# Audio tower on one core: the second chunk's tokens and first norm inside the first chunk's scan, and norm steps ahead of scans

## The reference

```python
h = einsum('bnp,dp->bnd', patches, W) + b                 # tokens
x = layernorm(h)                                          # "ln1"
u = rmsnorm(x, rms1_w) @ in_proj_w.T                      # z, xv, B, C, dt_in
dt = softplus(dt_in @ dt_proj_w.T + dt_proj_b)
dA = exp(dt[..., None] * A); dBx = (dt * x_full) * B
for each step: s = dA * s + dBx; y = C . s                # 10 steps, 16 states a channel
y = (y + D_skip * x_full) * silu(z)
r = x + y @ out_proj_w.T
h = h + r + (silu(rmsnorm(r) @ gate.T) * (rmsnorm(r) @ up.T)) @ down.T     # "rms2"
h = h + (silu(ln(h) @ wg.T) * (ln(h) @ wu.T)) @ wd.T                       # "ln2"
```

## Time and profile before

| | us |
|---|---|
| median of 3 runs | 675.78 (672.87 to 676.73) |
| the profiled execution, its own time | 675.06 |
| its span in the profile | 673.3 |
| PE busy in the span | 631.5 |
| POOL, DVE, ACT busy | 429.2, 418.0, 346.4 |

### The profile page before, as it was taken

How to read it: one execution, slowest core, us unless ns; L and a number is a source line. 1 busy time by engine, 2 the same in 40 slices (tenths; PEclk the granted TensorE clock), 3 DMA queues, 4 the chain that set the end, 5 groups by cost and what they waited for, 6 DMA issues and landing times.

```text
span 673.3 us, 8617 instructions
## 1 busy us (share of the span) xinstructions
PE 631.5 (94%) x2846; PEld 505.7 (75%) x2846; DVE 418.0 (62%) x532; ACT 346.4 (51%) x773; POOL 429.2 (64%) x244
## 2 busy tenths in 40 slices
PE   4969998799999989999979999999999999999998
PEld 3736765466665757777747777766999998999998
DVE  4077896889887879889887888851322223332132
ACT  4359889358989364434356433422542442653441
POOL 0176785437786999987877987644455463445461
PEclk9879998799999989999989999999999999999999
DMA  8699997489999969988866898533443453134421
GB/s 340 238 365 364 318 299 268 141 258 357 350 373 348 390 250 349 413 336 318 320 247 257 320 330 323 191 125 122 138 149 126 125 157 126 63 130 132 146 67 44
DMA packets 49164, 163.50 MB, mean 243 GB/s; under 512 B 4320, under 2 KB 18528, under 8 KB 48480
## 3 DMA queue, kind: packets, MB, share of 16 engines
q1 hardware_dynamic: 49120, 162.95, 68.9%
HBM read 145.24 MB, written 17.69 MB: 242 GB/s over the span
## 4 chain that ended last, share of the span: by engine, by line
PE 75%; DVE 11%; ACT 5%; POOL 3%; issue 3%; DMA 2%; SPq 0%; DVEq 0%; ACTq 0%; POOLq 0%
PE work L992 54%; PE da L992 15%; DVE da L784 6%; PE work L1002 5%; DVE hs L794 3%; POOL hs L447 2%; ACT L522 2%; ACT da L548 1%; DMA bb<-b_rows 1%; DMA c_rows<-c_rows 1%; DMA sm<-small 0%; POOL hs L460 0%; DVE a L849 0%; ACT z L665 0%; DVE work L809 0%
## 5 line engine op out<-in xcount | busy, mean ns | idle before, releaser
L784 DVE TENSOR_TENSOR_SCAN da<-da,hs 128x580 f32<-128x580 f32 (+1 forms) x128 | 191.1, 1493 | 39.6 <-POOL hs L447 22.2
L447 POOL TENSOR_TENSOR hs<-dtx,bb 128x1160 f32<-128x1160 f32 (+1 forms) x64 | 171.2, 2677 | 61.1 <-PE work L1002 54.1
L426 POOL TENSOR_TENSOR ws<-wraw,ws 128x1024 fp32r<-128x1024 f32 x40 | 101.4, 2536 | 92.8 <-ACT ws L557 92.8
L992 PE MATMUL work<-sq,wraw 128*128 128x290 f32 x512 | 125.7, 406 | 1.1 <-DVE sq L882 1.1
L992 PE MATMUL work<-hn,win 128*128 128x290 f32 (+1 forms) x336 | 104.4, 459 | 16.6 <-DVE hn L857 8.1
L992 PEld LDWEIGHTS work<-sq,wraw 128*128 128x128 f32 x512 | 96.5, 189 | 30.0 <-issue 1.6
L548 ACT ACTIVATE da<-dt,a_neg 128x261 f32<-128x261 f32 (+1 forms) x256 | 118.2, 493 | 0.0
L794 DVE TENSOR_TENSOR hs<-da,cb 128x580 f32<-128x580 f32 (+1 forms) x128 | 105.2, 822 | 10.7 <-DMA cb<-c_rows 2.7
L992 PEld LDWEIGHTS work<-hn,win 128*128 128x128 f32 x336 | 65.5, 200 | 50.7 <-issue 26.0
L545 ACT COPY da<-zeros 128x58 f32<-128x58 f32 (+1 forms) x128 | 27.6, 216 | 126.0 <-DVE hs L794 125.8
L557 ACT CAST ws<-wraw 128x1024 fp32r<-128x1024 f32 x48 | 50.3, 1048 | 70.2 <-PE da L992 34.4
(11 more groups left out here) (98 smaller groups left out, 655.2 us busy)
## 6 DMA issues: line engine op xcount, KB each, us to landing
wraw<-w_stream SPq DMA_DIRECT2D x104, 512.0 KB, 4.1
bb<-b_rows SPq DMA_DIRECT2D x32, 700.0 KB, 7.1
cb<-c_rows SPq DMA_DIRECT2D x32, 700.0 KB, 5.6
bb<-b_rows SPq DMA_DIRECT2D x32, 580.0 KB, 8.0
cb<-c_rows SPq DMA_DIRECT2D x32, 580.0 KB, 6.0
c_rows<-c_rows SPq DMA_DIRECT2D x8, 875.0 KB, 10.8
c_rows<-c_rows SPq DMA_DIRECT2D x8, 725.0 KB, 6.6
win<-w_in SPq DMA_DIRECT2D x4, 1024.0 KB, 13.4
```

The source lines that it names most:

```text
L426: nc.gpsimd.tensor_tensor(ws[:, k % NW, 1, :], wraw[:, split_loads[k] % NRAW, :], ws[:, k % NW, 0, :].bitcast(F32), ALU.subtract).then_inc ...
L447: nc.gpsimd.tensor_tensor(hs[:, u % NH, 0:NQ * n].rearrange("p (n t) -> p n t", t=n), dtx[:, t % 2, 0:n].unsqueeze(1).to_broadcast([P, NQ, ...
L784: nc.vector.tensor_tensor_scan(da[:, j, 0:w], da[:, j, 0:w], hs[:, u % NH, j * w:(j + 1) * w], 0.0, ALU.mult, ALU.add).then_inc(scan_done, 1)
L992: last = nc.tensor.matmul(dst, w, x, start=(k == 0), stop=(k == len(pairs) - 1))
```

## The change

- Chunk 1's tokens are four steps of one product each, in slots 5, 6, 8 and 9, at the front of slots that hold chunk 0's projections; `mean` is put into slot 10, `ln1` into 11, `rms1` into 13. All but `rms1` are now `LATE`. The squares are kept in `th` and `acc`, which are idle in chunk 0's scan, the norm's results in `rstd` and `rstd_ln`, so that neither `sq` nor a PSUM bank is held.
- Slots 14 to 16 now hold `in_dt`, `in_b`, `in_x`; slots 17 to 28 chunk 1's tiles 0 to 5; slots 29 to 31 `dtp`, `xs` and `in_z` of tile 6, one each. Of what slot 32 held, only this is left out; `in_c` of tile 6 moves to slot 36, `in_z` of tile 7 to 37, `dtp` and `in_c` of tile 7 to 50 and 51. In slots 12 and 13 the steps of chunk 0's tile 7 change places.
- Beside the second scan ACT does the squares and the inverse root ahead of the next unit's decays, and DVE has places given by number (`PLACE`) for `out`, `rms2`, `ln2_mean` and `ln2_var`.

The plan of steps:

```diff
+def tokens(c):
+    return [("tok", c, k) for k in range(KD)]
...
-    bg += [[("dtp", 0, 7), ("in_c", 0, 7)], [("xs", 0, 7), ("in_z", 0, 7)]]
-    bg += [[("tokc", 1)], [("mean", 1), ("ln1", 1)], [("rms1", 1)], [("in_dt", 1), ("in_b", 1, 0)],
-           [("in_x", 1, 0), ("in_b", 1, 1)], [("in_x", 1, 1)]]
+    bg += [[("in_c", 0, 7), ("in_z", 0, 7)], [("dtp", 0, 7), ("xs", 0, 7)]]
+
+
+    for u, s in zip((5, 6, 8, 9, 10, 11, 13), tokens(1) + [("mean", 1), ("ln1", 1), ("rms1", 1)]):
+        bg[u].insert(0, s)
+    bg += [[("in_dt", 1), ("in_b", 1, 0)], [("in_x", 1, 0), ("in_b", 1, 1)], [("in_x", 1, 1)]]
     bg += two_tiles(1, 0) + two_tiles(1, 2) + two_tiles(1, 4)
+    bg += [[("dtp", 1, 6)], [("xs", 1, 6)], [("in_z", 1, 6)]]
...
-    first = [[("dtp", 1, 6), ("in_c", 1, 6), ("xs", 1, 6)], [("xs", 1, 7)], o[0:2], o[2:4]]
+    first = [[], [("xs", 1, 7)], o[0:2], o[2:4]]
...
-        rest += {"rms2": [("in_c", 1, 7), s, ("in_z", 1, 6)], "ln2_mean": [s, ("in_z", 1, 7)],
-                 "ln2_var": [s, ("dtp", 1, 7)]}.get(s[0], [s])
+        rest += {"rms2": [("in_c", 1, 6), s, ("in_z", 1, 7)], "ln2_mean": [s, ("dtp", 1, 7)],
+                 "ln2_var": [s, ("in_c", 1, 7)]}.get(s[0], [s])
...
-LATE = ("dtp", "xs", "in_c", "in_z", "out")
-SEAM = (("in_c", 1, 7), ("in_z", 1, 6), ("in_z", 1, 7), ("dtp", 1, 7))
+LATE = ("dtp", "xs", "in_c", "in_z", "out", "tok", "mean", "ln1")
+SEAM = (("in_c", 1, 6), ("in_z", 1, 7), ("dtp", 1, 7), ("in_c", 1, 7))
+
+PLACE = {("out", 0, 2): 2, ("out", 0, 3): 2, ("rms2", 0): 2, ("ln2_mean", 0): 1, ("ln2_var", 0): 0}
```

Token and norm on ACT, with the buffers:

```diff
+        def token_square(c, k):
+            if c == 0:
+                return sq[:, k, 0:TS[c]]
+            return (th[:, k, :] if k < 2 else acc[:, (k - 2) * TM:(k - 1) * TM])[:, 0:TS[c]]
...
+                if kind == "tok":
+                    k = s[2]
+                    if (c, k) == (0, 0):
                         act.wait_ge(tokb_done, 1)
-                    else:
...
+                    full(act, s)
+                    nc.scalar.activation(a(c, k), bank(s), ACT.Identity, bias=tok_bc[:, k:k + 1]).then_inc(centered, 1)
+                    nc.scalar.activation(token_square(c, k), bank(s), ACT.Square,
+                                         bias=tok_bc[:, k:k + 1]).then_inc(free_of(s), 1)
...
                     log_tables()
-                    if v >= 1:
-                        act.wait_ge(norm_done, KD * v)
...
-                    act.wait_ge(h_done, KD * (c + 1))
-                    nc.scalar.activation(bank(("mean", c)), ln, ACT.Exp, scale=-0.5).then_inc(rstd_done, 1)
+                    if c == 0:
+                        act.wait_ge(h_done, KD * (c + 1))
+                        nc.scalar.activation(bank(("mean", c)), ln, ACT.Exp, scale=-0.5).then_inc(rstd_done, 1)
+                    else:
+                        nc.scalar.activation(ln, ln, ACT.Exp, scale=-0.5).then_inc(rstd_done, 1)
...
-                    var = ("ln1", c)
+                    var = bank(("ln1", c)) if c == 0 else rstd[:, 0:n]
...
-                    link(nc.scalar.activation(rstd[:, 0:n], bank(var), ACT.Ln, bias=eps_ap))
-                    nc.scalar.activation(bank(var), rstd[:, 0:n], ACT.Exp, scale=-0.5).then_inc(rstd_done, 1)
+                    link(nc.scalar.activation(rstd[:, 0:n], var, ACT.Ln, bias=eps_ap))
+                    nc.scalar.activation(var, rstd[:, 0:n], ACT.Exp, scale=-0.5).then_inc(rstd_done, 1)
...
+                    if c >= 1 and kind == "in_x":
+                        full(act, ("xs", c - 1, KI - 1))
+                    if c >= 1 and kind == "in_b":
+                        act.wait_ge(b_stored, 16 * 2 * c)
+                    if c >= 1 and kind == "in_dt":
+                        full(act, ("dtp", c - 1, KI - 1))
```

ACT's order beside the second scan:

```diff
-                    norm = [s for s in steps if s[0] in ("rms2", "ln2_var")]
-                    if norm:
-
-                        n = steps.index(norm[0])
-                        between = [steps[n - 1]] if steps[n - 1] == SEAM[2] else []
-                        first = steps[:n - len(between)] + [("squares",) + norm[0]]
-                        second = between + [("root",) + norm[0]] + steps[n + 1:]
+
+                    if i + 1 < len(slots) and ("rms2", 0) in slots[i + 1][1]:
+                        second.insert(0, ("squares", "rms2", 0))
+                    if ("rms2", 0) in steps:
+                        first, second = [("root", "rms2", 0)], [s for s in steps if s[0] != "rms2"]
+                    if ("ln2_mean", 0) in steps:
+                        first = [("squares", "ln2_var", 0), ("root", "ln2_var", 0)]
+                        second = [s for s in steps if s[0] != "ln2_mean"]
+                    if ("ln2_var", 0) in steps:
+                        first, second = [], [s for s in steps if s[0] != "ln2_var"]
```

DVE and PE:

```diff
+                    if c >= 1:
+                        dve.wait_ge(h_done, KD * (c + 1))
+                        dve.sem_inc(free_of(s), 1)
...
-                    nc.vector.tensor_tensor(bank(s), bank(s), rstd[:, 0:n], ALU.mult).then_inc(scaled_var, 1)
+                    nc.vector.tensor_tensor(bank(s) if c == 0 else rstd[:, 0:n], bank(s), rstd[:, 0:n],
+                                            ALU.mult).then_inc(scaled_var, 1)
+                    if c >= 1:
+                        dve.wait_ge(scaled_var, c + 1)
+                        dve.sem_inc(free_of(s), 1)
                     dve.wait_ge(rstd_done, NORMS.index(s) + 1)
                     for k in range(KD):
-                        nc.vector.tensor_tensor(a(c, k), a(c, k), bank(("mean", c)), ALU.mult).then_inc(norm_done, 1)
+                        nc.vector.tensor_tensor(a(c, k), a(c, k), bank(("mean", c)) if c == 0 else rstd_ln[:, 0:n],
+                                                ALU.mult).then_inc(norm_done, 1)
...
-                                                       in1=bank(var), op0=ALU.mult, op1=ALU.mult).then_inc(norm_done, 1)
+                                                       in1=bank(var) if c == 0 else rstd[:, 0:n],
+                                                       op0=ALU.mult, op1=ALU.mult).then_inc(norm_done, 1)
...
+                    for s in reversed([s for s in others if s in PLACE]):
+                        parts.insert(PLACE[s], s)
+                    others = [s for s in others if s not in PLACE]
...
-                    for k in range(KD):
-                        product(("tokc", c, k), [(tokw[:, k * P:(k + 1) * P], pat[:, OFF[c]:OFF[c] + n])])
+                    product(s, [(tokw[:, s[2] * P:(s[2] + 1) * P], pat[:, OFF[c]:OFF[c] + n])])
...
-                    product(s, [(mean_w[:, :], sq[:, k, 0:n], free_of(("tokc", c, k)), uses[("tokc", c, k)][1] + 1)
+                    product(s, [(mean_w[:, :], token_square(c, k), free_of(("tok", c, k)), uses[("tok", c, k)][1] + 1)
```

26 lines of the change are left out of this document (8 added, 18 removed).

## The result

The changed kernel takes 681.96 us (median of 4 runs, 681.27 to 682.82), the kernel before, run beside it, 675.0; the ratio is 1.0094, 95% interval 1.0067 to 1.0121. It is slower, by 6.3 us by the ratio (7.0 by the medians), where 17.5 us less were forecast. The profiled execution has a span of 681.0 us.

The account below looks back on a forecast made before the run. The chain of waits was taken as the bound, with no engine full in units 5 to 13. Gains of 7 (first scan), 4.5 (rms2) and 6.4 (ln2) sum to 17.9: 675.06 becomes 657.2, median 657.5; range 652 to 667.

Parts of the forecast that it names:

- No engine is full: Units 5 to 13: four units take 19.19 us, DVE busy 17.31 and ACT 15.39, so added work finds room.
- rival C: Units 6 to 13: three-bank ring makes PE, POOL, DVE and ACT wait in a circle, 24 us lost, 681.5; chance 0.05.
- The norm on VectorE: Units 11 to 13: 6.2 us of DVE work plus waits of 2.1 and 2.2; unit 14 begins at 115.4, not 105.01.
- Rival A: First scan returns nothing: unit 14 begins 17 us later instead of 10.4, only the seams gain, 664.5; chance 0.16.
- PE needs 89.1 us from there: From in_dt to unit 29's sums: 77.3 us now plus 11.8 of moved work, ending at 203.3, 2.6 us earlier.
- PE ... is the bound: PE sets the time from in_dt to the sums of unit 29, 77.3 us in the kernel before.
- The C rows need not be late: one store less stands in SP's queue.: Ahead of the output projection: the 2.65 us wait for C rows need not occur; if it does, 2.65 come back.
- Rival D: No change: seams and first norm gain nothing net, units wait for something unseen such as DMA, 675; chance 0.05.
- DVE would allow it: First scan: from 115.4, 18 units of 4.22, four gates of 0.93 and unit 32 give 200 for unit 33.
- rms2, 4.5 us: Output projection to first gu: 27.2 us becomes 22.7, gain 4.5, or 1 to 2 less if either cover fails.
- ln2, 6.4 us: At ln2, gu starts at 347.6 against 354.51, 6.9 sooner, 0.5 lost as PE waits for DVE; net 6.4.
- rival B: Beside the MLPs DVE becomes the bound, norm steps delay units 38 and 52, ln2 returns 3, 661; chance 0.10.

Follow-up runs that it names:

- products_twice: Kernel before, with six TensorE products issued twice into the same bank in slots 5, 6 and 8 to 11, nothing else added: 678.01 us, ratio 1.0038.
- warm_both: weights_later with 12 idle TensorE products of 128 rows ahead of the output projection and 4 ahead of chunk 1's in_dt: 672.92 us, ratio to before 0.9968.
- weights_later: Changed kernel with its six weight loads (3.1 MB) issued five slots later on the DMA queue: 677.86 us, ratio to before 1.0039.
- warm_out: weights_later with 12 idle TensorE products of 128 rows in the wait ahead of the output projection: 675.04 us, ratio to before 1.0006.
- tokens_behind: Changed kernel with the seven token and norm steps last in their slots instead of first, behind the state sums: 682.88 us, ratio to before 1.0108.
- clock_kept: weights_later with 13 idle TensorE products of 32 rows in the wait ahead of the output projection: 678.72 us, ratio to before 1.0062.

## Why the prediction was wrong, point by point

Four steps of the sum failed most. TensorE was taken to have room in units 5 to 13; the norm's four products on VectorE were priced too low; behind the sums of unit 29 the C rows and VectorE's scans were taken to be on time (8.6 us); and at ln2 0.5 us were taken to be lost where it was 4.4. In order:

*"No engine is full" in units 5 to 13.* This failed, and it was there to read: in the earlier trace rows PE is busy 18.96 of 19.19 us, and the sentence named only VectorE and ScalarE. So the tokens were priced on ScalarE (1.2 us) and their products, with the mean and the variance 5 x 0.59 + 2.36 = 5.3 us by the earlier trace rows, on nobody. `products_twice` prices 4.4 us of such work at 0.65 us by unit 10, 2.6 us by unit 13 and about 60% at the end. The changed kernel has lost 2.8 us by unit 10, where its chain goes through banks that ScalarE reads late, as rival C describes; no run parts that from ScalarE's and TensorE's added work.

*The norm on VectorE.* The waits were right (2.14 and 1.98). The term of 2.2 us for lines 846 and 849 was mis-sized: with rstd in SBUF the four products of 849 take 4.1 to 5.3 us instead of 1.8. Under "what costs nothing" the prediction asked what the shared interface costs GpSimd, which had time, and not what it costs VectorE, which had none. Rival A names this place with 17 us; 15.4 were measured, from unit 1 to unit 14 (79.3 us for 63.9), with 10.4 forecast. Of the 5.0 between, 2.6 fall into unit 12 with these products, 1.6 ahead of unit 10, and 0.5 into unit 13.

*The clock at `in_dt`.* The prediction hoped that it would stay up behind 1.7 us of waiting; the wait was 2.71 and `in_dt` took 5.01 us. Against the kernel before this is a gain that did not come and not a loss, since the clock was as low there. In seven of the eight profiles with the changed first part, no cover and the C rows loaded as before, `in_dt` ran at the lower level for most or all of its 8 records (4.17 to 5.01 us), behind waits of 1.94 to 4.05 us, once at full clock (2.60) behind 2.70. Price 2.1 us by the medians (`warm_both`).

*"PE needs 89.1 us from there".* Short by 2.6: the sums of unit 29 are the first half of the 16 records from 209.80 on, and end at 211.8, 91.7 us behind 120.14. The clock is not the reason, since the 77.3 us of before hold it too. The prediction moved three units' sums behind `in_dt`; it is four. PE does the sums of unit u - 2 in slot u, behind the first half of its steps, but ahead of all of them where u % 4 is 1. So before they stand in front of `in_dt` in slot 17 and the first sums behind it are unit 16's (14 groups to unit 29), while in slot 14 they stand behind `in_dt` and are unit 12's (18 groups). That is 1.96 us more, and 0.5 for the first of them at the lower clock.

*"PE ... is the bound" to the sums of unit 29.* The chain of the kernel before does not say so. It leaves TensorE 11 us earlier, at the sums of unit 27, for the gate and the scans of VectorE:

```profile
192.80 1.97 PE work L1002 x8
...
194.87 0.54 DVE work L809
...
195.80 1.38 DVE da L784
```

The next piece of TensorE in it starts at 209.89. The step "POOL's multiply 3.0, two scans and multiplies 5.0, gate 1.0" behind the sums of 29 therefore followed a path that was not the last to end.

*"The C rows need not be late: one store less stands in SP's queue."* Wrong, and with the path just named the costliest step: `out` starts 17.6 us behind the sums of unit 29 instead of 9.0. The stores were counted and the weight loads were not, though they hang on a step that the diff moves; each queue a step is moved past has to be followed. `weights_later` prices them at 4 us: there `out` starts 13.4 us behind those sums, and the other 4.4 us stay with VectorE. Late rows in units 20 to 33 are among the prediction's own signs of being wrong. Rival D had DMA as a reason for no change, at 0.05.

*"DVE would allow it", 200 us for unit 33.* Also too low. With rows on time (`warm_both`) unit 33 starts at 214.69; taking off the 5.2 us by which unit 14 is later than forecast leaves 209.5. Units 15 and 16 take 5.17 and 6.33 us instead of 4.22, and the gates behind units 21, 25 and 29 cost 2.1 to 3.5 instead of 0.93, since they wait for TensorE's sums (2.1 us in two of them). So TensorE holds VectorE back up to the gate behind unit 29, and from there VectorE's scans set the end. TensorE runs dry ahead of `out`, and its clock falls: `out` takes 2.9 us longer in the changed kernel, 1.6 in `weights_later`, where covering it lowers the median by 2.8 (`warm_out`). No step of the prediction has this.

*rms2, 4.5 us.* The mechanism was right (22.4 us to the first `gu` for 22.7), the size not: 3.4 us are left at unit 50 (118.4 for 121.9), since TensorE waits 1.1 us for VectorE behind the first `gu`. In the changed kernel the 2.9 us of the clock took most of this.

*ln2, 6.4 us.* The 6.9 us to the first `gu` were exact. "0.5 lost" was the mis-sized term: 4.4 were lost, 2.5 are left. VectorE reads the first gate 9.5 us behind the first `gu`, because ScalarE has softplus, three pairs of decays, a copy of C and a table load ahead of the tanh, and the last decays wait for VectorE. The chain stays on VectorE up to 379.83. That is rival B, which said 3.

*Rival C.* That its 681.5 is what was measured is chance. Its circle is there, as the chain in units 6 to 9 shows, and behind unit 1 GpSimd makes VectorE's scans wait three times up to unit 10 (2.5 us, 0.4 before). But it costs at most 2.8 us by unit 10, not 24, and `tokens_behind` undoes the order that it blames and gains nothing. The rest of the loss comes from the other places named here.

*The sum.* 675.06 - 17.9 is 657.2; with the 0.7 us of the median it is 657.9, not 657.5, which changes nothing. After the three repairs of `warm_both` 14.5 us of the forecast are still missing by the table: 4.8 in the head, 4.8 up to `out`, 1.0 at rms2 and 4.0 at ln2.

## What to carry to other kernels

Read every column of the window before saying that no engine is full, the DMA share too: work moved "into a gap" must be priced on each engine that it runs on and each queue whose triggers it moves. A start that comes sooner is worth only what the next bound lets through; here VectorE and DMA took back more than `in_dt` had won, and TensorE's clock added to it. Follow the chain of waits to the point that a sum is meant to reach, and count the work between two points from the rows on both sides of them. And a seam gains no more than the time until the engine behind it runs dry.

## What the runs showed of the hardware

VectorE with both operands in SBUF takes 4.1 to 5.3 us instead of 1.8 for four products of 128x350 while GpSimd works, with and without a scalar; with one operand in PSUM it is not slowed (1.80). The granted clock fell to 0.50 while TensorE worked through 14 products of 32 rows (`clock_kept`), and stayed at 1.00 beside 12 products of 128 rows in the same place (`warm_out`). Behind a wait of 2.70 us the clock was full in one execution (`clock_kept`) and half in another behind 2.71 (the changed kernel), and unit 15 lasted 5.23 and 8.15 us. Over a stretch of the first scan all transfers together ran at 157 GB/s with a DMA share of 0.50 where the C rows came by a load whose outer dimension repeats, at 293 GB/s (1.03) where four loads read the same rows, and at 345 GB/s (1.01) where the rows are stored several times.
